# R turned in 32x32 squares on VectorE, the triangular solve in 32x64 tiles, and one filler product less in a recurrent attention and expert kernel

## What is computed

```python
def step(s, inp):
    q_, w_, k_, v_, a_, b_ = inp
    sa = jnp.einsum('bhij,bhj->bhi', s, a_)
    s = s * w_[:, :, None, :] + sa[..., None] * b_[:, :, None, :] + v_[..., None] * k_[:, :, None, :]
    return (s, jnp.einsum('bhij,bhj->bhi', s, q_))
```

## Time and profile before

| | |
|---|---|
| median of 3 runs | 1091.34 us (1085.73 to 1097.99) |
| the profiled execution | 1092.08 us |
| its span, first to last instruction | 1090.1 us |
| TensorE clock granted, mean | 0.97 |
| PE / PEld / DVE / ACT / POOL busy | 93 / 76 / 71 / 50 / 56% |

### The profile page before, as it was taken

One profiled execution on the slowest core, in us unless ns is written; L12 is line 12 of the kernel. 1 busy time (PEld: TensorE's weight loads), 2 busy tenths in 40 slices (PEclk: granted clock), 3 DMA queues, 4 the chain that ended last, 5 costly groups with the idle time before them and its releaser, 6 DMA issues.

```text
span 1090.1 us, 42536 instructions
## 1 busy us (share of the span) xinstructions
PE 1016.1 (93%) x16804; PEld 833.7 (76%) x16805; DVE 778.8 (71%) x1777; ACT 542.1 (50%) x1113; POOL 612.6 (56%) x1135
## 2 busy tenths in 40 slices
PE   8898999999999999999999999679899999999995
PEld 5675777787776776777777777566798888989894
DVE  4775887888787977888878877247566666666663
ACT  4474676686585775766766757222122222222220
POOL 1087786787776875877868868640223232323321
PEclk9998999999899998999999999689999999999998
DMA  4113224134133242242251341838454454545430
GB/s 104 41 20 79 71 35 107 42 71 107 25 89 90 33 100 60 52 109 57 56 106 28 86 100 18 234 86 289 179 184 165 163 180 153 186 146 181 147 127 4
DMA packets 208625, 112.02 MB, mean 103 GB/s; under 512 B 172365, under 2 KB 191953, under 8 KB 208081
## 3 DMA queue, kind: packets, MB, share of 16 engines
q1 hardware_dynamic: 202080, 100.77, 34.3%
q0 software_dynamic: 3744, 8.40, 2.3%
q10 hardware_dynamic: 2640, 0.54, 0.2%
HBM read 85.42 MB, written 26.08 MB: 102 GB/s over the span
## 4 chain that ended last, share of the span: by engine, by line
PE 80%; DMA 5%; DVE 4%; issue 4%; POOL 3%; ACT 1%; SPq 1%; DVEq 0%; POOLq 0%; ACTq 0%
PE bank L561 20%; PE bank L950 12%; PE bank L963 9%; PE bank L699 6%; PE bank L646 6%; PE bank L654 5%; PE ry L963 4%; PE bank L607 4%; PE ry L676 3%; PE ry L728 2%; PE bank L716 2%; PE ry L682 2%; POOL arena L1906 2%; POOL arena L1903 2%; PE bank L579 1%
## 5 line engine op out<-in xcount | busy, mean ns | idle before, releaser
L1906 POOL TENSOR_TENSOR arena<-arena 128x30 f32<-128x30 f32 (+14 forms) x480 | 258.9, 539 | 37.6
L1903 POOL TENSOR_TENSOR arena<-arena 128x30 f32<-128x30 f32 (+14 forms) x480 | 252.8, 527 | 36.4
L561 PE MATMUL bank<-arena 128*128 128x256 f32 (+2 forms) x992 | 267.3, 406 | 4.9 <-DVE arena L1405 2.4
L561 PEld LDWEIGHTS bank<-arena 128*128 128x128 f32 x992 | 171.2, 194 | 49.5 <-issue 25.1
L950 PEld LDWEIGHTS bank<-arena 128*128 128x128 f32 x1248 | 145.3, 192 | 5.5 <-issue 2.7
L950 PE MATMUL bank<-arena 128*128 128x128 f32 x1248 | 145.8, 275 | 3.2 <-DVE arena L1812 2.5
L1489 DVE TENSOR_TENSOR arena<-bank,arena 128x512 f32<-128x512 f32 x128 | 79.6, 684 | 34.1 <-PE bank L646 34.1
L1293 ACT ACTIVATE arena<-arena 128x1 f32<-128x1 f32 x39 | 11.5, 295 | 176.5 <-DVE arena L1766 176.5
L963 PE MATMUL bank<-arena 128*128 x416 | 96.4, 385 | 0.1
L1937 POOL COPY arena<-arena 128x1 int32 (+1 forms) x39 | 7.1, 183 | 144.8 <-DVE arena L1830 144.8
L963 PEld LDWEIGHTS bank<-arena 128*128 128x128 f32 x416 | 76.9, 190 | 14.4 <-issue 4.9
(11 more groups left out here) (174 smaller groups left out, 1806.8 us busy)
## 6 DMA issues: line engine op xcount, KB each, us to landing
arena<-in_W SPq DMA_DIRECT2D x47, 1024.0 KB, 5.0
scr_n<-arena SPq DMA_DIRECT2D x64, 128.0 KB, 2.7
arena<-scr_n SPq DMA_DIRECT2D x16, 512.0 KB, 4.0
scr_u<-arena SPq DMA_DIRECT2D x16, 512.0 KB, 2.9
arena<-scr_u SPq DMA_DIRECT2D x62, 128.0 KB, 2.9
arena<-in_xTp SPq DMA_DIRECT2D x32, 132.0 KB, 4.0
arena<-in_x SPq DMA_DIRECT2D x64, 64.0 KB, 2.2
scr_x<-arena SPq DMA_DIRECT2D x64, 64.0 KB, 2.7
```

Of the source, the lines that this page charges most:

```text
L561: mm = pe.matmul(ring.tile(m, name)[0:rows, to], lhsT, rhs, start=(i == 0), stop=(i == len(terms) - 1))
L1903: inv_ok.inc(f"m{s}", TT(t, U[:, 0:s, s:s + 1].broadcast_to(shape), U[:, s:s + 1, s + 1:TB].broadcast_to(shape), ALU.mult))
L1906: inv_ok.inc(f"a{s}", TT(U[:, 0:s, s + 1:TB], U[:, 0:s, s + 1:TB], t, ALU.add))
```

## The change

- **Transpose.** keep_r no longer masks: it writes R with two VectorE transposes, which turn each 32x32 square (32 channels of a pair by 32 steps) into `Rs`. turn_r (8 transposes on TensorE) and keep_rt (2 copies of 128x512 on ScalarE) go.
- **Solve.** A product now has 32 rows (the steps), 64 columns (two heads of 32 steps) and the pair's 32 channels moving; there are still 64 of them per block. solve(m, w) takes pairs 2w and 2w + 1 of both halves; pair 2w goes to bank "xa", pair 2w + 1 to "xb", and four successive products use four different tiles. The inverse is stored with the steps on 32 partitions per pair, without zero blocks, still by four transfers.
- **Mask.** What a product gives for the wrong head is zeroed on the way out: three masked copies of 64x512 on VectorE (two from "xa", one from "xb"), and two scaled copies of half that size on ScalarE ("xb"). Before it was two plain copies of 64x512 on each.
- **Places.** On TensorE, solve(n - 1, 0) now stands where turn_r stood, in front of project_out(n - 2), and it is the one that waits for the transfers of `Ux`; solve(n - 1, 1) stays behind project_out. read_out and update now wait for all of X. update(n - 1, 1) moves in front of scores(n + 1, 0). On ScalarE the copies of X move in front of keep_keys(n, 1, 1). The layouts in DRAM follow, and one small mask more is loaded at the start.
- **Filler.** The keep_busy in bodies 3 to 14 goes.

The core of the diff:

```diff
-                            (-2, "g@0"), (1, "ma@5 mk@2"), (-1, "rt0@3 rt1@4"), (-2, "wo@0"), (-1, "x1@1"),
-                            (1, "ss@0 r@4"), (0, "bk11@5"), (1, "v@2"), (-1, "x0@3"), (0, "bk10@5 v0@1 v1@4"),
+                            (-2, "g@0"), (1, "ma@5 mk@2"), (-1, "xa@1 xb@3"), (-2, "wo@0"),
...
+        def solution_home(m, q, e):
+            return XV[m % 2][x_rows_of(e), e:NB:2, :].rearrange("p g (w q i) -> p w q g i", w=2, q=2)[:, :, q]
+
+        def solution(m, bank, e):
+            return ring.tile(m, bank)[x_rows_of(e), :].rearrange("p (w g i) -> p w g i", w=2, g=NB // 2)
+
+        u_rows = ud.rearrange("(g q) (r c) -> g r q c", g=PAIRS, r=TB)
+        pair_rows = lambda p: slice(32 * p, 32 * p + 32)
+        heads_of = lambda m, p: Ux[m % 2][pair_rows(p)].rearrange("r k f e h t -> r (k f e h) t")
...
-                for e in range(2 if m < last else 1):
-                    for h in range(2):
-                        at_row = 64 * (1 - e) + TB * h
-                        sp.dma_start(Ux[m % 2][at_row:at_row + TB, :, :, :, h, :], u_rows[e, h]).then_inc(u_in, 16)
-
-            u_rows = ud.rearrange("(f g k e h) (r c) -> e h r f g k c", f=HALF, g=PAIRS, k=4, e=2, r=TB)
+                    ring.wait_full(sp, m - 2, "xa", "xb")
+                for p in range(PAIRS if m < last else 2):
+                    sp.dma_start(heads_of(m, p), u_rows[p]).then_inc(u_in, 16)
...
-            def turn_r(m, f):
-                chain_dve.wait(pe, m, "rme", "rmo")
-                turn(m, f"rt{f}", [Rm_flat[:, (f * 4 + k) * P:(f * 4 + k + 1) * P] for k in range(4)])
-
-            def solve(m, f):
-                ring.wait_empty(pe, m, f"x{f}")
-                chain_act.wait(pe, m, f"rt{f}")
-                pe.wait_ge(u_in, (m + 1) * 64)
-                for k in range(B // 2):
-                    for p in range(PAIRS):
-                        for e in range(2):
-                            x, at = x_rows_of(e), k * P + 32 * p
-                            mm = pe.matmul(ring.tile(m, f"x{f}")[x, at:at + 32], Ux[m % 2][x, f, p, k].rearrange("p h t -> p (h t)"),
-                                           RT[f][x, k, 32 * p:32 * p + 32], start=True, stop=True)
-                ring.fill(m, f"x{f}", mm)
-
-            def x_kept(m, f):
-                chain_act.wait(pe, m, f"x{f}e")
-                chain_dve.wait(pe, m, f"x{f}o")
+            def solve(m, w):
+
+                if w == 0:
+                    for bank in "ab":
+                        ring.wait_empty(pe, m, f"x{bank}")
+                    chain_dve.wait(pe, m, "re", "ro")
+                    pe.wait_ge(u_in, (m + 1) * 64)
+                else:
+                    pe.wait_ge(half_solved, m + 1)
+                mm = {}
+                for g in range(NB // 2):
+                    for turn in range(2):
+                        for i, bank in enumerate("ab"):
+                            e, r = (turn + i) % 2, pair_rows(2 * w + i)
+                            at = (w * NB // 2 + g) * 32
+                            mm[bank] = pe.matmul(ring.tile(m, f"x{bank}")[x_rows_of(e), at:at + 32],
+                                                 Ux[m % 2][r, g % 4, g // 4, e].rearrange("p h t -> p (h t)"), Rs[r, e, g, :],
+                                                 start=True, stop=True)
+                if w == 1:
+                    for bank in "ab":
+                        ring.fill(m, f"x{bank}", mm[bank])
+                else:
+                    mm["b"].then_inc(half_solved, 1)
+
+            def x_kept(m):
+                chain_act.wait(pe, m, "xb0", "xb1")
+                chain_dve.wait(pe, m, "xae", "xao", "xbo")
...
-                if 2 < n < last:
-                    ring.wait_empty(pe, n - 3, "logit")
-                    keep_busy(1, ring.tile(n - 3, "logit"))
...
-                if has(n - 1):
-                    turn_r(n - 1, 0)
-                    turn_r(n - 1, 1)
+                if has(n - 1) and n - 1 < last:
+                    solve(n - 1, 0)
...
-                if has(n - 1):
-                    solve(n - 1, 0)
...
+                if has(n - 1) and n - 1 < last:
+                    update(n - 1, 1)
...
-            def keep_x(m, f, e):
-                ring.wait_full(act, m, f"x{f}")
-                x = x_rows_of(e)
-                chain_act.inc(m, f"x{f}{'eo'[e]}", A(XV[m % 2][x, f * B + e:(f + 1) * B:2, :],
-                                                     ring.tile(m, f"x{f}")[x, :].rearrange("p (k n) -> p k n", k=4), ACT.Copy))
+            def keep_x(m):
+                ring.wait_full(act, m, "xb")
+                x = x_rows_of(0)
+                for h in range(2):
+                    i = slice(HS * h, HS * h + HS)
+                    chain_act.inc(m, f"xb{h}", A(solution_home(m, 1, 0)[:, :, :, i], solution(m, "xb", 0)[:, :, :, i], ACT.Copy,
+                                                 scale=own_head[x, h:h + 1]))
...
-                shape = [P, NB // 2, 2, TB]
+                    ring.wait_full(dve, m - 1, "xa", "xb")
                 for e, name in enumerate("eo"):
-                    chain_dve.inc(m, f"rm{name}", TT(Rm[:, :, 1 - e], RY[e][:, :, 0, None, :].broadcast_to(shape),
-                                                     odd_even[:, None, :, None].broadcast_to(shape), ALU.mult))
-
-            def keep_x_odd(m, f):
-                ring.wait_full(dve, m, f"x{f}")
-                x = x_rows_of(1)
-                chain_dve.inc(m, f"x{f}o", nc.vector.tensor_copy(XV[m % 2][x, f * B + 1:(f + 1) * B:2, :],
-                                                                 ring.tile(m, f"x{f}")[x, :].rearrange("p (k n) -> p k n", k=4)))
+                    chain_dve.inc(m, f"r{name}", nc.vector.transpose(Rs[:, e], RY[e][:, :, 0]))
+
+            def keep_x(m, bank, e):
+                ring.wait_full(dve, m, f"x{bank}")
+                chain_dve.inc(m, f"x{bank}{'eo'[e]}", TT(solution_home(m, "ab".index(bank), e), solution(m, f"x{bank}", e),
+                                                         same_head[x_rows_of(e), None, None, :].broadcast_to([P // 2, 2, NB // 2, 32]),
+                                                         ALU.mult))
...
-                    keep_x_odd(n - 1, 1)
+                    keep_x(n - 1, "a", 0)
+                    keep_x(n - 1, "a", 1)
...
-                    keep_x_odd(n - 1, 0)
+                    keep_x(n - 1, "b", 1)
```

More of the change, by code:

```diff
@@ L239, in build @@
         Ux_flat = take(2 * HALF * PAIRS * 4 * 2 * TB)
-        Ux = [v.rearrange("p (f g k h t) -> p f g k h t", f=HALF, g=PAIRS, k=4, h=2)
-              for v in (Ux_flat[:, 0:2048], Ux_flat[:, 2048:4096])]
+        Ux = [v.rearrange("p (k f e h t) -> p k f e h t", k=4, f=HALF, e=2, h=2)
+              for v in (Ux_flat[:, 0:1024], Ux_flat[:, 1024:2048])]
         at_rm = top[0]
-        Rm_flat = take(NB // 2 * P)
-        Rm = Rm_flat.rearrange("p (g o h t) -> p g o h t", g=NB // 2, o=2, h=2)
-        RT = [take(4 * P).rearrange("p (k n) -> p k n", k=4) for _ in range(HALF)]
+        Rs = take(NB * TB).rearrange("p (e g i) -> p e g i", e=2, g=NB // 2)
+        head_mask = take(TB + 2)
+        same_head, own_head = head_mask[:, 0:TB], head_mask[:, TB:TB + 2]
+        take(3 * DEPTH * D - 2 * NB * TB - (TB + 2))
         S = take(NB * TB).rearrange("p (g i) -> p g i", g=NB)
@@ L361, in build @@
         freed.update({f"v{f}": [(turned, f"v{f}e"), (turned, f"v{f}o")] for f in range(HALF)})
-        freed.update({f"x{f}": [(chain_act, f"x{f}e"), (chain_dve, f"x{f}o")] for f in range(HALF)})
+        freed["xa"] = [(chain_dve, "xae"), (chain_dve, "xao")]
+        freed["xb"] = [(chain_act, "xb0"), (chain_act, "xb1"), (chain_dve, "xbo")]
         filled = [sem(f"filled{i}") for i in range(len(banks))]
         ring = Ring(banks, [(0, "bk00@5"), (1, "h@2 k@3"), (0, "bk01@2"), (1, "z@1 a@4 kk@5"), (-3, "logit@2"),
[2 rows of a table removed]
[2 rows of a table added]
                             (1, "rk@3"), (-1, "su@0"), (1, "sc00@2 sc01@5 sc02@3 sc03@1 tg@4"), (2, "lo1@5"),
@@ L722, in read_out @@
                 buf = m % 2
-                x_kept(m, f)
+                x_kept(m)
                 for b in range(B):
@@ L822, in body @@
                 if n == last + 1:
-                    ring.wait_empty(pe, last, "x1")
+                    ring.wait_empty(pe, last, "xa")
                     keep_busy(2, idle_ps)
+                if n - 1 == last:
+                    solve(n - 1, 0)
                 if has(n - 1):
@@ L872, in body @@
                     warm_up(2)
-                if has(n - 1) and n - 1 < last:
-                    update(n - 1, 1)
                 if has(n + 1):
@@ L1197, in keep_logits, with second_inverse_to_heads @@
                                         ring.tile(m, "logit")[:, 0:16].rearrange("p (j e) -> p j e", e=8), ACT.Copy))
-            def odd_inverse_to_heads(m):
+            def second_inverse_to_heads(m):
                 act.wait_ge(u_out, (m + 1) * 16)
```

(18 more changed lines are left out.)

32 lines of the change are left out of this document (14 added, 18 removed), and 1 row of the table ring.

## The result

The changed kernel takes 1209.7 us (median of four runs, 1203.5 to 1220.1) where the kernel before takes 1093.7 (four runs, 1085.7 to 1098.0). The ratio is 1.111, 95% interval 1.105 to 1.117: **slower by 11%**. The sign was forecast, the size was not: 1118 us is +2.4%, and the time lies far outside the range.

The account below looks back on a forecast made before the run. The loop through TensorE's wait for Ux, SP's fixed 17.5 us and VectorE's chain was taken to bound the changed kernel at 43.2 us a body: 1092.1 + 5 + 21.5 (clock) = 1118.6, forecast 1118 us, range 1078 to 1138.

Parts of the forecast that it names:

- SP's way: From last masked score to Ux landing, through SP's transfers: a fixed lag of 17.5 us, none of it TensorE's work.
- the faster rival: Ux is in time because SP's way is shorter, deciding at 17.1 us; 1078 or 1048 us; chance 0.16.
- the other half of the loop: The chain from Ux landing to the last masked score: 25.7 us, closing the loop at 43.2 with SP's 17.5.
- the rival of two tiles: In the solves only two of four tiles overlap: 2.0 us each, 13 us more, 1131 us; chance 0.12.
- The clock behind the first wait: Clock falls behind the Ux wait, slowing solve and project_out: 2.2 us in three bodies of four, +21.5 us.
- the sum: Profiled 1092.1 us plus 5 for the longer loop plus 21.5 for clock falls: 1118.6, taken as 1118.
- the sign I gave: What would show the forecast right: among others, TensorE idle at read_out until VectorE's last copy of X.
- update(1) only changes its place inside it: Between read_out and the second scores' start: moving update(1) leaves that stretch at 8.3 us.
- the undisturbed body: One body of the kernel before without disturbance, 40.9 us against 42.8 per body over 12, used for the chain's times.
- The second slow rival: A second clock fall, behind 2.3 us of waiting at read_out before small tiles: +11 to +22 us; chance 0.12.
- I count none of it on either side: Short holes and slow clock stretches in the old body's 42.8 us: some fall into the new waits, priced at nothing.

Follow-up runs that it names:

- 3: The kernel before with one added line: TensorE waits for Ux in front of turn_r and project_out; 3.6% slower.
- 6: The changed kernel with only update(n - 1, 1) back in front of scores(n + 1, 1); gives back 3.6 us per body.
- 8: The kernel before with only update(n - 1, 1) moved in front of scores(n + 1, 0); 1143 us against 1098, 4.4% slower.
- 7: The changed arithmetic (VectorE transposes, 32x64 tiles, masked copies) with every TensorE step at its old place, filler kept; 1111 us, 1.3% slower than the kernel before.
- 9: The kernel before with update(n - 1, 1) moved and two unread products in front of it; 19 us faster than the same kernel without those products.
- 5: The changed kernel with the first solve behind project_out and update(n - 1, 1) back at its old place; 4.9 points less than with the solve moved alone.
- 1: The changed kernel with solve(n - 1, 0) behind project_out(n - 2) instead of in front; 7.4% slower than the kernel before, 47.4 us per body against 51.1.

## Why the prediction was right in sign and wrong in size

**Right as written.** The first solve waits for `Ux` behind nothing of TensorE's own (2.98 us at 456.99, 2.2 on the mean of 13 bodies; forecast 3.1), and VectorE idles ahead of add_tokens, longer than forecast: 1.82 us in the body shown (at 410.09), 4.8 on the mean, forecast 2.9. SP's way is a fixed lag: 17.1 us on the mean of 13 bodies, forecast 17.5. That is the very point from which the faster rival was to decide, and the time is nowhere near it, because the other half of the loop grew. The solve's 64 records run from 409.91 to 410.98: 1.07 us, forecast 1.05, so the rival of two tiles falls. The Trainium skill's rule that was weighed there ("TensorE: Matmul & The Clock Gate", section "The mechanism") would have left the solve near 2 us; this number contradicts it for 32x64 tiles. The transposes take 0.422 us each, less than the 0.64 of the products that they replace; no run prices them apart:

```profile
L1501 DVE STREAM_TRANSPOSE arena<-ry x32: 405/422/450, 90.6 to 841.7; 128x256 f32<-128x256 f32 x32
```

**The clock behind the first wait** was priced about right: from the landing of `Ux` to add_tokens' start the mean is 5.2 us, forecast 3.1 + 0.75 x 2.2 = 4.75. To read_out it is 15.5, forecast 12.9 + 1.65 = 14.6. Of the 0.9 between them 0.4 is there at add_tokens already, and the way from add_tokens over the last copy of X to read_out took the rest (10.3 us, forecast 9.8). In time the early wait alone costs 3.6%, 39 us (3), where the sum has 26.5 for the wait and the clock together. TensorE doesn't wait at read_out for it, as the sign I gave says, but ahead of it, by pieces: 0.96 at 415.23 and 1.16 at 419.22, for the rows of VectorE (L1408, L1428) that stand in front of that copy.

**The step that failed** is "update(1) only changes its place inside it", in the chain from read_out to the second scores. It was costed at nothing. Read_out to the last masked score was forecast at 8.3 + 4.5 = 12.8 us and takes 18.7. A body before takes 14.2 on the mean (the 12.8 was the undisturbed body), so 1.4 was missed by taking one good body. Of the other 4.5, putting the update back (6) gives 3.7, and moving it in the kernel before (8) costs 3.7. Priced at 3.6 us per body, 13 bodies, it is 47 us. The evidence stood in rows 3 and 6: read_out and update at 0.76 us for 64 records are the densest instructions of the body, and the 4.26 us at 712.99 end in "issue" in the middle of just such a group. I read that hole as a wait that the clock falls behind, and didn't ask what it waited for: counted as above, it lies 769 instructions behind the hole before it and ends 1.3 us after such a transfer. A second term was put at nothing by leaving it out: who waits for the banks of X once its copies and its order change (1.3%, 14 us, by 7).

**What follows from it.** The second slow rival had the right observation (a second fall in the small tiles) for the wrong reason (the wait at read_out) and at most 22 us. With a loop that is set by the chain from `Ux` to `Ux`, each us of a late score comes back as a us per body: 34.2 + 17.1 = 51.3 us, and 51.1 is the body. "I count none of it on either side", for the short holes and slow stretches of the old body, had the same fault: they don't hide in the waits when the chain runs through them.

**What stays open.** How much of the moved update's 3.6 us is the hole and how much the clock that falls behind it: 9 removes both together. Which of the edits between 5 and 7 makes their 1.2%, the second solve's place, the copies' or the filler, is open too. Not tried: gate_1 in the row with a bank that is free there, and X in banks that are full behind one solve each.

## What to carry to other kernels

A step that waits for a transfer belongs behind all work that doesn't need it: in front of project_out the wait for `Ux` cost 3.0 to 3.7 us a body (3, 1), slow clock included; behind it the kernel before waits for it 3.8 us in all 14 bodies. Before moving a short product group, count the instructions of the unbroken run that it joins, and compare the run's instructions per us with the supply that the holes marked "issue" betray. When a bank's contents or the engine that empties it change, look for its next tenant: the 1.8 us a body that "xa" was held ate all that the faster solve saved.

## What the runs showed of the hardware

- TensorE's instructions arrive in transfers of 16384 bytes that start at least 3.3 us apart. Of the changed kernel's 28 holes of 0.7 to 2.6 us marked "issue", 27 lie multiples of 256 instructions apart, within one, most of them in runs of 64-record groups that take 0.7 us. The kernel before has the 3.3 us too (the nearest starts are 3.35 us apart in both).
- The granted clock can fall behind a hole so short: after one of 1.57 us at 424.69 the stretch from 426.4 to 440.0 ran at 0.50, after 1.00 in the 26.4 us before it, in which TensorE had waited 1.03, 0.96 and 1.16 us:

```profile
400.00:426.40 26.40, 21.67 (x508) 17.07 (x507) 21.07 (x38) 19.98 (x38) 23.58 (x37) 1.00 0.26 51
426.40:440.00 13.60, 13.02 (x201) 9.88 (x199) 6.91 (x12) 3.26 (x8) 7.26 (x18) 0.50 0.14 23
```

- Four tiles in turn gain also where two of them share their rows: 64 records of 32x64 tiles take 1.07 us, of two 64x64 tiles in turn 1.98.
- VectorE turns 128x256 in 32x32 squares in 0.42 us (median of 32), against 0.64 for a product of 128x512.
